# Order of the window sums and the turned maxima, and bank pairs of the score blocks, in an attention and convolution kernel on Trainium2

## The chip, the cores and the metric

The kernel runs on one core of one Trainium2 chip. TensorE (PE), VectorE (DVE), ScalarE (ACT), GpSimd (POOL) and SyncE (SP, which issues the transfers) each work through a queue of their own in program order and meet at semaphores. The metric is the device time of one launch in microseconds, the median of the runs.

## The reference, cut to what matters

```python
x = x + attention(gn(x))       # x is (4, 256, 32, 32): 4 images, 256 channels
x = x + conv(gn(x))

# attention: two halves of 128 channels
qkv = (windows(xh) @ h_qkv_w)                  # hifi: 2x2 windows, 4 tokens each, 4 heads of 32
attn = softmax(einsum('bghnd,bghmd->bghnm', q, k) * SCALE)      # 4 x 4 scores per window and head
hifi = einsum('bghnm,bghmd->bghnd', attn, v) @ h_proj_w + h_proj_b
q = xh @ l_q_w                                 # lofi: 1024 queries against 256 pooled keys, 4 heads
k, v = mean_2x2(xh) @ l_kv_w
lofi = softmax(q @ k.T * SCALE) @ v @ l_proj_w + l_proj_b

# conv: mask from each channel's centre of mass, then 3x3, 256 -> 256 channels
conv(x) = conv3x3(relu(x * mask(x)), weight) + bias
```

`gn` normalises over groups of 8 channels.

## The kernel before

The four images go through the same program one after the other. For image `b` the functions `front(b)` and `rest(b)` of each engine follow one another; the convolution of image `b-1` runs inside the attention of the next images: `Convolution(b).more(n)` issues the next `n` of its matmuls wherever TensorE would otherwise wait. The numbers of these matmuls stand in the tables `FRONT` and `REST`. `FRONT[2 + n]` come behind score block `n`, `FRONT[10]` (6) and `FRONT[11]` (10) around the window sums, `FRONT[12]` (23) behind the first pooled scores. Images 0 and 1 have no convolution to put there yet; in image 1 `keep_warm` issues filler matmuls behind blocks 5, 6 and 7 (6, 1 and 2 of them, two rows each in the trace).

The results of TensorE go to PSUM, which has four bank pairs here: `cps`, used by the convolution, and `slot[0]` to `slot[2]`, shared by all else. Each use of a pair waits by a semaphore until the reader of the one before is done.

The part that matters is the second half of `front(b)`:

- **Score blocks.** For each of 8 blocks of 128 queries TensorE makes the scores of 4 heads against 256 keys (L1185, four matmuls of 256 columns, `slot<-ks,qs` in the trace) into `slot[LA_SLOT[n]]`. VectorE takes the maxima over the keys (L782, `l_max<-slot`) and counts `la_max` up. Block `n` waits for the maximum that frees its pair.
- **Turned maxima.** TensorE transposes `l_max` (L1196, into `slot[2]`), VectorE copies it in two parts (`maxima_parts`, L790 and L792), and SyncE sends both to rows of `qs` (L280), where the pooled scores (`slot<-qs,ks`) need them.
- **Window sums.** GpSimd multiplies queries and keys of the windows (L348, `probs<-q_w,k_w`), TensorE sums the products over each head's channels (`window_scores`, `slot<-probs,cst`, 8 matmuls, 16 rows in the trace), ScalarE copies the sums (L542, `q_w<-slot`), TensorE transposes them (L1206, 8 transposes), and VectorE starts the softmax (`window_softmax`, L799 to L806) whose weights are turned back (L1229), copied by ScalarE as `p_w` (L556) and used for the values.
- **Convolution input of image `b-1`.** VectorE multiplies with the mask (`masked_image`, L722), ScalarE rectifies (L503, `rectify`), VectorE makes the tiles `v` (`conv_tiles`, L736 to L744) and their low parts (`conv_low`, L752, `v_lo`), ScalarE the high parts (L514, `v_hi`). TensorE's next convolution waits for both.

VectorE's order in `front` (L844) is written by hand: eight maxima, `maxima_parts`, a result of the older convolution, the two masked images, the first tiles, and then the window softmax.

Of the kernel before, what the change touches and what calls it, by code (L numbers as in the profile page):

```python
# [13 lines left out]
P = 128  # L14
B, C, H, W = 4, 256, 32, 32
KT = C // P
# [6 lines left out]
HEADS, HD = 4, 32  # L23
# [5 lines left out]
NB = HW // P  # L29
# [13 lines left out]
C_ID, C_GRP, C_HEAD, C_ONE = 0, P, 2 * P, 2 * P + HD  # L43
# [8 lines left out]
SPLITS = (slice(WLQ, WLK), slice(WLK, WCOLS), slice(WQ, WLQ))  # L52


LA_SLOT = (0, 1, 2, 0, 1, 2, 0, 1)
ST_SLOT = (0, 1, 0, 1, 1, 0, 2, 1)
PB_SLOT = (0, 1, 0, 2)

# [44 lines left out]
def build(nc, x, wqkv, whp, wlp, bh, bl, cw, cb, mw, filt, consts, selectors, out):  # L103
    with ExitStack() as ctx:
# [306 lines left out]
        def _(act):  # L411
# [23 lines left out]
            def input_moments(b, i):  # L435

                for k in range(KT):
                    act.wait_ge(x_in[b][k], 16)
                    channel_moments(b, 0, k, probs[:, i + k])
# [83 lines left out]
            def step(b, first, last):  # L523
                if first:
                    act.wait_ge(w_in, 3 * KT * 16)
                    nc.scalar.copy(w_hi[:], raw_w).then_inc(w_split, 1)
                    normalise_first()
                late = b + 1 == RING
                projections(b, first)
                if first:  # L530
                    act.wait_ge(cw_dve, CW_DVE)
                    weight_high(0, V_SUM, 2)
                    weight_high(0, V_DIFF, 0)
                if not first:
                    normalise_y(b - 1, b + 1)
                if not last and not late:
                    act.wait_ge(stacked_late, (b + 1) * STACK_LATE)
                    input_moments(b + 1, 0)
                if not first:
                    rectify(b - 1, 0)  # L540
                act.wait_ge(ssum_pe, b + 1)
                nc.scalar.copy(q_w[:], flat_cps if first else flat[0]).then_inc(ssum_sb, 1)  # L542
                if not first:
                    rectify(b - 1, 1)
                act.wait_ge(soft_c, b * N_SOFT + SOFT_READ)
                nc.scalar.activation(s_exp, s_exp, ACT.Exp, scale=SCALE).then_inc(sexp, 1)
                if not first:
                    conv_high(b - 1, 0)
                if not last and not late:
                    act.wait_ge(moments[0], (b + 2) * KT)  # L550
                exp_scores(b, range(2))
                if not first:
                    conv_high(b - 1, 1)
                    exp_scores(b, range(2, LT - NW))
                act.wait_ge(pt_pe, b + 1)
                nc.scalar.copy(p_w[:], flat[2]).then_inc(pt_act, 1)  # L556
                if first:
                    exp_scores(b, range(2, LT - NW))
                    act.wait_ge(cw_pool, CW_TURNED)
                    weight_high(1, V_SUM, 2)  # L560
                    weight_high(1, V_DIFF, 0)
                if late:
                    input_moments(b + 1, LT - NW)
                    act.wait_ge(moments[0], (b + 2) * KT)
                exp_scores(b, range(LT - NW, LT))
                if not last:
                    normalise(b + 1)
# [24 lines left out]
        def _(dve):  # L592
# [193 lines left out]
            def maxima_parts(b):  # L786

                dve.wait_ge(lmt_pe, b + 1)
                rows = slot[2][0:NB * HEADS, 0, 0:P]
                nc.vector.tensor_copy(lm_hi, rows).then_inc(lm_dve, 1)  # L790
                dve.wait_ge(lm_dve, b * 2 + 1)
                nc.vector.tensor_tensor(lm_lo, rows, lm_hi.bitcast(F32), ALU.subtract).then_inc(lm_dve, 1)  # L792
# [208 lines left out]
        def _(pe):  # L1001
# [120 lines left out]
            def front(b, conv, first=False):  # L1122

                starting = not first and isinstance(conv, NoConvolution)

                def tile_ready(k):
                    pe.wait_ge(xhi_ready, b * KT + k + 1)
                    pe.wait_ge(xlo_ready, b * KT + k + 1)


                project(slot[0], WLQ, tile_ready)
                if starting:
                    keep_warm(WARM[10])
                pe.wait_ge(pool_c, (b + 1) * N_POOL)
                if not first:
                    pe.wait_ge(y_ready, b * KT - 1)
                if first:
                    pe.wait_ge(w_split, 3)
                for k in range(KT):
                    split_mm(slot[1][:, 0, 0:G], (w_hi[:, k, WLK:WLK + P], w_lo[:, k, WLK:WLK + P]),  # L1140
                             (pool_hi[:, k], pool_lo[:, k]), k == 0, k == KT - 1)
                for t in range(MT):
                    m = slice(t * P, (t + 1) * P)
                    for k in range(KT):
                        ins = split_mm(slot[1][:, 1, m], (pool_hi[:, k, m], pool_lo[:, k, m]),
                                       (w_hi[:, k, WLV:WLV + P], w_lo[:, k, WLV:WLV + P]), k == 0, k == KT - 1)
                ins.then_inc(proj_pe, 1)
                if first:
                    pe.wait_ge(w_split, 4)
                else:  # L1150
                    pe.wait_ge(y_ready, b * KT)
                project(slot[2], WQ)
                pe.wait_ge(lq_dve, b + 1)
                project(slot[0], WK)
                conv.more(FRONT[0])
                if not first:
                    wait_count(pe, conv_out, (b - 2) * EVENTS + POS)
                    group_means(b - 1, 1)
                if not first:
                    pe.wait_ge(lk_act, (b + 1) * 2)  # L1160
                    pe.wait_ge(lk_dve, b + 1)
                    project(slot[1], WV)
                else:
                    project(cps, WV)
                conv.more(FRONT[1])

                for n in range(NB):
                    if n == 0:
                        pe.wait_ge(stacked, (b + 1) * STACK)
                        pe.wait_ge(qkv_sb, b * 3 + 2)  # L1170
                    elif n == 1:
                        if first:
                            pe.wait_ge(lk_act, 2)
                            pe.wait_ge(lk_dve, 1)
                        else:
                            pe.wait_ge(qkv_sb, b * 3 + 3)
                    elif n == 2:
                        if not first:
                            pe.wait_ge(gn_c[1], (b - 1) * N_GN + 1)
                    else:  # L1180
                        pe.wait_ge(la_max, b * NB + n - 2)
                    if n == NB // 2:
                        pe.wait_ge(stacked_late, (b + 1) * STACK_LATE)
                    for h in range(HEADS):
                        ins = mm(flat[LA_SLOT[n]][:, h * G:(h + 1) * G], qs[0:SC, h, n * P:(n + 1) * P], ks[0:SC, h],  # L1185
                                 True, True)
                    ins.then_inc(la_pe, 1)
                    conv.more(FRONT[2 + n])
                    if starting:
                        keep_warm(WARM[1 + n])  # L1190
                if first:
                    pe.wait_ge(qkv_sb, 3)
                    window_scores(b, cps)
                    pe.wait_ge(zeroed, 1)
                pe.wait_ge(la_max, (b + 1) * NB)
                nc.tensor.transpose(slot[2][:, 0, 0:P], l_max[:], cst[:, C_ID:C_ID + P]).then_inc(lmt_pe, 1)  # L1196
                conv.more(FRONT[10])
                if not first:
                    window_scores(b, slot[0])
                conv.more(FRONT[11])  # L1200

                pe.wait_ge(ssum_sb, b + 1)
                if not first:
                    pe.wait_ge(lm_dve, (b + 1) * 2)
                for n in range(NB):
                    ins = nc.tensor.transpose((cps if first else slot[2])[:, n // 4, (n % 4) * P:(n % 4 + 1) * P],  # L1206
                                              q_w[:, n * P:(n + 1) * P], cst[:, C_ID:C_ID + P])
                ins.then_inc(stok_pe, 1)

                if first:  # L1210
                    pe.wait_ge(ones, 1)
                pe.wait_ge(max_stacked, (b + 1) * MAX_STACK)
                for i in range(2):
                    pooled_scores(b, i)
                conv.more(FRONT[12])
                if not first:
                    Convolution(b - 1).more(EARLY)
# [155 lines left out]
```

## Time and profile before

| | us |
|---|---|
| median of 3 runs | 368.33 (368.22 to 368.52) |
| profiled execution | 366.82 |
| its span, first to last instruction | 364.9 |
| TensorE busy | 322.0 (88%) |
| VectorE busy | 280.5 (77%) |
| ScalarE busy | 148.0 (41%) |
| GpSimd busy | 85.8 (24%) |

The profiled execution took 1.9 us more than its span, and 1.5 us less than the median. Times in the rows below are from the start of the span. A matmul's row shows its modelled end, so rows of one engine overlap; the step from start to start is its pace. The mean granted clock of TensorE was 0.949 of full speed. Image 0's score blocks stand at 32 to 43 us, image 1's at 95 to 110, image 2's at 173 to 186 and image 3's at 249 to 261.

### The profile page before, as it was taken

How to read it: one execution, taken by the hardware profiler on the slowest of the kernel's cores; microseconds unless marked ns; L12 is line 12 of the kernel's file. 1: busy time of each engine (PE TensorE's matmuls, PEld its weight loads, DVE VectorE, ACT ScalarE, POOL GpSimd, SP SyncE). 2: the span in 40 equal slices, each digit the busy share in tenths (PEclk: the TensorE clock that was granted, in tenths of full speed). 3: DMA queues.
4: the chain of work that ended last, by engine and by line, in shares of the span. 5: the costliest groups of instructions: out<-in, count | busy, mean ns of one | idle time of the engine just before them, and what ended most of it. 6: DMA issues, size and time to landing. Idle time of an engine off the chain costs nothing.

```text
span 364.9 us, 4118 instructions
## 1 busy us (share of the span) xinstructions
PE 322.0 (88%) x1546; PEld 227.9 (62%) x1546; DVE 280.5 (77%) x518; ACT 148.0 (41%) x186; POOL 85.8 (24%) x47
## 2 busy tenths in 40 slices
PE   1786864999797699998999999998999999979995
PEld 1375542257564485486868773786777836858884
DVE  4979839777867957789897877988879847997662
ACT  2443556345443635535215764453048333031300
POOL 0464948000192020000760020005900200202000
PEclk9999698799968599999899999998999999999999
DMA  8659700007900000029510300098001000101002
GB/s 266 259 81 129 238 5 0 2 0 98 118 2 4 0 2 1 0 82 129 63 38 25 115 3 0 2 169 105 2 4 57 3 0 0 59 0 57 2 0 117
DMA packets 10340, 20.39 MB, mean 56 GB/s; under 512 B 1872, under 2 KB 4816, under 8 KB 10064
## 3 DMA queue, kind: packets, MB, share of 16 engines
q1 hardware_dynamic: 10320, 20.13, 26.8%
q8 instruction: 12, 0.20, 0.2%
q14 instruction: 8, 0.07, 0.1%
HBM read 7.93 MB, written 4.19 MB: 33 GB/s over the span
## 4 chain that ended last, share of the span: by engine, by line
PE 58%; DVE 17%; DMA 8%; ACT 6%; issue 4%; SPq 2%; POOL 2%; DVEq 0%
PE slot L1003 26%; PE cps L1035 16%; PE slot L1079 7%; DMA ks<-probs 4%; PE cps L1003 4%; DMA qs<-probs 3%; ACT probs L520 2%; PE cps L1079 2%; SPq L257 1%; DVE v_lo L752 1%; DVE xn L979 1%; SPq L261 1%; DVE l_max L782 1%; DMA xy<-x 1%; PE slot L1206 1%
## 5 line engine op out<-in xcount | busy, mean ns | idle before, releaser
L348 POOL TENSOR_TENSOR probs<-q_w,k_w 128x1024 f32<-128x1024 f32 x16 | 38.4, 2428 | 115.7 <-DVE rw L715 110.5
L1035 PE MATMUL cps<-v_hi,cw_hi 128*128 128x512 f32 (+1 forms) x144 | 58.6, 407 | 3.8 <-DVE v_lo L752 3.6
L1035 PE MATMUL cps<-v_hi,cw_lo 128*128 128x512 f32 (+1 forms) x144 | 58.4, 406 | 0.0
L1035 PE MATMUL cps<-v_lo,cw_hi 128*128 128x512 f32 (+1 forms) x144 | 57.4, 398 | 0.0
L782 DVE TENSOR_REDUCE l_max<-slot 128x4 f32<-128x1024 f32 x32 | 37.6, 1219 | 7.2 <-PE slot L1003 7.2
L520 ACT ACTIVATE probs<-slot 128x1024 f32<-128x1024 f32 x32 | 31.9, 1023 | 16.8 <-PE slot L1003 16.7
L1035 PEld LDWEIGHTS cps<-v_hi,cw_hi 128*128 128x128 f32 x144 | 28.3, 197 | 14.2 <-ACT v_hi L514 4.3
L1003 PE MATMUL slot<-ks,qs 96*128 96x256 f32 x128 | 24.9, 343 | 10.5 <-DVE l_max L782 4.4
L1035 PEld LDWEIGHTS cps<-v_hi,cw_lo 128*128 128x128 f32 x144 | 28.0, 194 | 6.3 <-issue 0.7
L1035 PEld LDWEIGHTS cps<-v_lo,cw_hi 128*128 128x128 f32 x144 | 28.1, 195 | 4.9
L1003 PEld LDWEIGHTS slot<-ks,qs 96*128 96x128 f32 x128 | 21.8, 236 | 14.4 <-DVE l_max L782 6.7
L503 ACT ACTIVATE xn<-mask 128x1024 f32<-128x1024 f32 x8 | 8.5, 1058 | 45.5 <-DVE mask L722 45.5
L1003 PE MATMUL slot<-xn_hi,w_hi 128*128 128x512 f32 x60 | 24.7, 411 | 2.3 <-DVE xn_lo L650 2.3
L333 POOL TENSOR_TENSOR mask<-rw 128x1024 f32<-128x1024 f32 x8 | 15.2, 1915 | 44.3 <-DVE rw L715 44.3
L1003 PE MATMUL slot<-qs,ks 98*128 98x512 f32 x64 | 21.0, 421 | 5.1 <-ACT probs L520 3.5
L514 ACT CAST v_hi<-mask 128x1024 fp32r<-128x1024 f32 x16 | 16.8, 1049 | 21.0 <-DVE mask L744 11.8
L1003 PE MATMUL slot<-xn_hi,w_lo 128*128 128x512 f32 x60 | 23.9, 398 | 0.0
L1003 PE MATMUL slot<-xn_lo,w_hi 128*128 128x512 f32 x60 | 23.7, 394 | 0.0
L392 POOL TENSOR_TENSOR q_w<-q_w,k_w 128x1024 f32<-128x1024 f32 x3 | 7.2, 2416 | 67.2 <-DVE k_w L885 67.2
L1003 PE MATMUL slot<-probs,cst 128*32 128x512 f32 x176 | 22.8, 657 | 0.0
L752 DVE TENSOR_TENSOR v_lo<-mask,v_hi 128x1024 fp32r<-128x1024 f32 x16 | 19.2, 1224 | 2.3 <-ACT v_hi L514 2.3
L1003 PE MATMUL cps<-cst 128*128 128x384 f32 x44 | 19.7, 602 | 0.0
(188 smaller groups left out, 623.2 us busy)
## 6 DMA issues: line engine op xcount, KB each, us to landing
qs<-probs SPq DMA_DIRECT2D x24, 256.0 KB, 7.5
xy<-x SPq DMA_DIRECT2D x8, 512.0 KB, 8.1
out<-xy SPq DMA_DIRECT2D x8, 512.0 KB, 2.8
raw_cw<-conv_w SPq DMA_DIRECT2D x2, 1152.0 KB, 6.9
ks<-probs SPq DMA_DIRECT2D x12, 128.0 KB, 7.4
probs<-h_qkv SPq DMA_DIRECT2D x2, 192.0 KB, 4.5
probs<-l_kv SPq DMA_DIRECT2D x2, 128.0 KB, 3.9
probs<-selectors SPq DMA_DIRECT2D x1, 256.0 KB, 4.0
```

The costliest lines, as they stand in the source:

```text
L257: sp.dma_start(qs[HD * part:HD * (part + 1), :, n].bitcast(F32), parts[:, n].bitcast(F32)).then_inc(done, 16)
L333: nc.gpsimd.tensor_tensor(mask[:, k].rearrange("p (h w) -> p h w", h=H), rw[:, k, 0].unsqueeze(2).to_broadcast([P, H, W]), rw[:, k, 1].uns ...
L348: nc.gpsimd.tensor_tensor(qk[:, j].rearrange("p (n w) -> p n w", n=NW), q_w[:].rearrange("p (n w) -> p n w", n=NW), k_w[:, j * G:(j + 1) * ...
L392: nc.gpsimd.tensor_tensor(pv[0], pv[0], pv[1], ALU.add).then_inc(pv_pool, 1)
L503: nc.scalar.activation(xn[:, k], mask[:, k], ACT.Relu).then_inc(relu, 1)
L514: nc.scalar.copy(v_hi[:, k, 2 * phase:2 * phase + 2].rearrange("p a b -> p (a b)"), mask[:, k]).then_inc(v_act, 1)
L520: nc.scalar.activation(probs[:, i], flat[score_slot(b, i)], ACT.Exp, scale=SCALE / NW)\
L752: nc.vector.tensor_tensor(v_lo[:, k, part].rearrange("p a b -> p (a b)"), mask[:, k], v_hi[:, k, part].rearrange("p a b -> p (a b)").bitca ...
L782: nc.vector.tensor_reduce(l_max[:, bass.ds(n, HEADS, step=NB)], flat[LA_SLOT[n]].rearrange("p (h m) -> p h m", h=HEADS), AX_X, ALU.max, ne ...
L1003: return nc.tensor.matmul(dst, lhsT, rhs, start=start, stop=stop)
L1035: ins = nc.tensor.matmul(cps[:, pos % 2, y0 * WT:y1 * WT], (cw_hi, cw_hi, cw_lo)[part][:, k, pos, dy + 1, o * P:(o + 1) * P], (v_hi, v_lo, ...
L1079: ins = nc.tensor.matmul(last_bank(o, pos)[:, y0 * WT:y1 * WT], (cw_hi, cw_hi, cw_lo)[part][:, k, pos, dy + 1, o * P:(o + 1) * P], (v_hi, ...
```

## The change

Three things are put in another order or place.

- `LA_SLOT`: blocks 5, 6 and 7 use the pairs 0, 1, 0 instead of 2, 0, 1. `LA_FREE` gives for each block the count of maxima that it waits for: 4 instead of 3 for block 5, 5 instead of 4 for block 6, 6 instead of 5 for block 7. So these three wait for the maximum of the block two before instead of three before.
- TensorE makes the window sums right behind the last block's convolution matmuls, into `slot[2]`, which block 2 was the last to use, and without a wait for the maxima. The transpose of `l_max` comes behind them and `FRONT[10]`, into `slot[1]`. The wait for `lm_dve` ahead of the sums' transposes goes.
- ScalarE copies the sums ahead of both rectifications, instead of between them.

```diff
-LA_SLOT = (0, 1, 2, 0, 1, 2, 0, 1)
+LA_SLOT = (0, 1, 2, 0, 1, 0, 1, 0)
+LA_FREE = (0, 0, 0, 1, 2, 4, 5, 6)
...
-                if not first:
-                    rectify(b - 1, 0)
                 act.wait_ge(ssum_pe, b + 1)
-                nc.scalar.copy(q_w[:], flat_cps if first else flat[0]).then_inc(ssum_sb, 1)
-                if not first:
-                    rectify(b - 1, 1)
+                nc.scalar.copy(q_w[:], flat_cps if first else flat[2]).then_inc(ssum_sb, 1)
+                if not first:
+                    for k in range(KT):
+                        rectify(b - 1, k)
...
-                rows = slot[2][0:NB * HEADS, 0, 0:P]
+                rows = slot[1][0:NB * HEADS, 0, 0:P]
...
-                        pe.wait_ge(la_max, b * NB + n - 2)
+                        pe.wait_ge(la_max, b * NB + LA_FREE[n])
...
                 if first:
                     pe.wait_ge(qkv_sb, 3)
-                    window_scores(b, cps)
                     pe.wait_ge(zeroed, 1)
+                window_scores(b, cps if first else slot[2])
+                conv.more(FRONT[10])
                 pe.wait_ge(la_max, (b + 1) * NB)
-                nc.tensor.transpose(slot[2][:, 0, 0:P], l_max[:], cst[:, C_ID:C_ID + P]).then_inc(lmt_pe, 1)
-                conv.more(FRONT[10])
-                if not first:
-                    window_scores(b, slot[0])
+                nc.tensor.transpose(slot[1][:, 0, 0:P], l_max[:], cst[:, C_ID:C_ID + P]).then_inc(lmt_pe, 1)
                 conv.more(FRONT[11])
 
                 pe.wait_ge(ssum_sb, b + 1)
-                if not first:
-                    pe.wait_ge(lm_dve, (b + 1) * 2)
```

In images 2 and 3 TensorE's queue behind the last convolution matmul of block 7 (`cps<-v_...` are convolution matmuls, `slot<-cst,l_max` is the transpose of the maxima, `slot<-probs,cst` the window sums) read before:

```order
L1196 MATMUL slot<-cst,l_max 128x128
L1035 MATMUL cps<-v_hi,cw_hi 128x512
L1035 MATMUL cps<-v_lo,cw_hi 128x512
L1035 MATMUL cps<-v_hi,cw_lo 128x512
L1035 MATMUL cps<-v_hi,cw_hi 128x512
L1035 MATMUL cps<-v_lo,cw_hi 128x512
L1035 MATMUL cps<-v_hi,cw_lo 128x512
L1003 MATMUL slot<-probs,cst 32x512 x8
L1035 MATMUL cps<-v_hi,cw_hi 128x496
```

and reads now:

```order
L1003 MATMUL slot<-probs,cst 32x512 x8
L1035 MATMUL cps<-v_hi,cw_hi 128x512
L1035 MATMUL cps<-v_lo,cw_hi 128x512
L1035 MATMUL cps<-v_hi,cw_lo 128x512
L1035 MATMUL cps<-v_hi,cw_hi 128x512
L1035 MATMUL cps<-v_lo,cw_hi 128x512
L1035 MATMUL cps<-v_hi,cw_lo 128x512
L1197 MATMUL slot<-cst,l_max 128x128
L1035 MATMUL cps<-v_hi,cw_hi 128x496
```

The sums moved up past the transpose and the six matmuls; the nine further convolution matmuls behind each are the same. In image 1, without a convolution, TensorE's queue from block 6 on is, before (- and + mark what goes and comes; `cps<-cst` are filler matmuls, `slot<-cst,q_w` the transposes of the sums):

```order
 L1003 MATMUL slot<-ks,qs 128x256 x4
 L1003 MATMUL cps<-cst 128x384 x2
-L1196 MATMUL slot<-cst,l_max 128x128
 L1003 MATMUL slot<-probs,cst 32x512 x8
-L1206 MATMUL slot<-cst,q_w 128x128 x8
+L1197 MATMUL slot<-cst,l_max 128x128
+L1202 MATMUL slot<-cst,q_w 128x128 x8
 L1003 MATMUL slot<-qs,ks 128x512 x4
 L1035 MATMUL cps<-v_hi,cw_hi 128x512
```

Only the transpose of the maxima changed places with the sums. VectorE's queue is unchanged in every image. In image 2 it reads from the last maxima to the softmax, before and now:

```order
L782 TENSOR_REDUCE l_max<-slot 128x4 x2
L790 CAST probs<-slot 32x128
L792 TENSOR_TENSOR probs<-slot,probs 32x128
L817 SCALAR_TENSOR_TENSOR xy<-cps,cbias,xy 128x512
L722 SCALAR_TENSOR_TENSOR mask<-mask,xn 128x1024 x2
L736 TENSOR_TENSOR mask<-xn 128x512
L737 TENSOR_TENSOR mask<-xn 128x512
L799 TENSOR_REDUCE s_max<-slot 128x32
```

Nothing moved there: the copy of the turned maxima (L790, the row with the wait for their transpose) stays ahead of the masked images (L722), the tiles (L736, L737) and the softmax (L799).

## Rows read from the trace of the kernel before

**Rows 1.** The page's chain that ended last, its shares by engine.

```profile
PE 58%; DVE 17%; DMA 8%; ACT 6%; issue 4%; SPq 2%; POOL 2%; DVEq 0%
```

**Rows 2.** That chain in order of time: start us, us, what; images 1 and 2.

```profile
122.64 4.79 PE cps L1035 x12
...
196.61 0.69 DVE mask L736
...
206.26 1.02 ACT p_w L556
207.32 0.74 PE slot L1003 x2
```

**Rows 3.** Timeline of TensorE, image 2: start us, us, engine, line, what.

```profile
173.68 2.35 PE L1003 MATMUL slot<-ks,qs 96*128 96x256 f32 x12 [1.79 <-DMA ks<-probs]
...
186.41 0.38 PE L1035 MATMUL cps<-v_hi,cw_lo 128*128 128x496 f32 x1
186.99 0.33 PE L1196 MATMUL slot<-cst,l_max 128*128 128x128 f32 x1 [0.20 <-DVE l_max L782]
187.07 0.48 PE L1035 MATMUL cps<-v_hi,cw_hi 128*128 128x512 f32 x1
...
188.63 1.94 PE L1003 MATMUL slot<-probs,cst 128*32 128x512 f32 x16
190.50 0.49 PE L1035 MATMUL cps<-v_hi,cw_hi 128*128 128x496 f32 x1
...
192.84 1.04 PE L1206 MATMUL slot<-cst,q_w 128*128 128x128 f32 x8
...
199.85 0.40 PE L1035 MATMUL cps<-v_hi,cw_hi 128*128 128x512 f32 x1
```

**Rows 4.** Timeline of VectorE, image 2; in brackets the idle time before.

```profile
187.35 0.28 DVE L790 CAST probs<-slot 32x128 fp32r<-32x128 f32 x1 [0.42 <-PE slot L1196]
...
188.71 2.35 DVE L722 SCALAR_TENSOR_TENSOR mask<-mask,xn 128x1024 f32<-128x1024 f32 x2
191.05 0.69 DVE L736 TENSOR_TENSOR mask<-xn 128x512 f32<-128x512 f32 x1
...
193.92 0.29 DVE L799 TENSOR_REDUCE s_max<-slot 128x32 f32<-128x128 f32 x1 [1.57 <-PE slot L1206]
```

**Rows 5.** Timeline of all engines, image 0.

```profile
35.43 9.20 DVE L782 TENSOR_REDUCE l_max<-slot 128x4 f32<-128x1024 f32 x8
...
38.78 3.75 PE L1003 MATMUL slot<-ks,qs 96*128 96x256 f32 x16 [1.35 <-DMA qs<-probs]
...
42.46 3.03 PE L1003 MATMUL cps<-probs,cst 128*32 128x512 f32 x16
...
49.43 1.16 PE L1003 MATMUL slot<-qs,ks 98*128 98x512 f32 x4 [1.66 <-DMA qs<-probs]
...
50.63 1.82 POOL L374 TENSOR_TENSOR raw_cw<-raw_cw 128x768 f32<-128x768 f32 x1 [4.65 <-DVE k_w L806]
```

**Rows 6.** Timeline of all engines, image 1.

```profile
111.74 0.33 PE L1196 MATMUL slot<-cst,l_max 128*128 128x128 f32 x1
...
113.86 1.06 ACT L503 ACTIVATE xn<-mask 128x1024 f32<-128x1024 f32 x1 [8.50 <-DVE mask L722]
114.82 0.99 ACT L542 COPY q_w<-slot 128x1024 f32<-128x1024 f32 x1
...
117.40 0.29 DVE L799 TENSOR_REDUCE s_max<-slot 128x32 f32<-128x128 f32 x1 [1.16 <-PE slot L1206]
...
122.64 0.77 PE L1035 MATMUL cps<-v_hi,cw_hi 128*128 128x512 f32 x1 [3.57 <-DVE v_lo L752]
```

**Rows 7.** Windows: length, busy of PE, PEld, DVE, ACT, POOL, granted clock, DMA.

```profile
49.00:51.00 2.00, 1.55 (x8) 1.07 (x9) 1.42 (x5) 0.77 (x1) 0.37 (x1) 1.00 0.01 4
44.00:45.50 1.50, 1.50 (x13) 0.29 (x5) 0.63 (x1) 0.46 (x2) 1.50 (x2) 0.76 0.02 8
174.50:176.00 1.50, 1.50 (x9) 1.50 (x8) 1.46 (x3) 0.71 (x1) 0.80 (x1) 0.50 1.08 123
```

More of the change, by code:

```diff
@@ L538, in step @@
                     input_moments(b + 1, 0)
+                act.wait_ge(ssum_pe, b + 1)
+                nc.scalar.copy(q_w[:], flat_cps if first else flat[2]).then_inc(ssum_sb, 1)
                 if not first:
-                    rectify(b - 1, 0)
-                act.wait_ge(ssum_pe, b + 1)
-                nc.scalar.copy(q_w[:], flat_cps if first else flat[0]).then_inc(ssum_sb, 1)
-                if not first:
-                    rectify(b - 1, 1)
+                    for k in range(KT):
+                        rectify(b - 1, k)
                 act.wait_ge(soft_c, b * N_SOFT + SOFT_READ)
```

## Prediction, written before the changed kernel ran

> **What bounds the kernel now.** I read the chain that ended last first. TensorE has 58% of it and VectorE 17% [rows 1], so neither engine's mean busy share answers the question: the chain changes engine inside every image, and the place where it changes is what counts. Followed in order of time through image 2 (images count from 0) it goes from TensorE over to VectorE (the softmax, then the second half of the convolution tiles at 196.61), from there to ScalarE (the turned weights' copy p_w at 206.26) and back to TensorE at 207.32 [rows 2]. What delays VectorE's softmax in an image therefore delays the end, one for one, until the end of p_w.
>
> Next I read the timeline of the two engines in that stretch. TensorE issues back to back: it waits 0.20 us for the last maximum before the transpose of l_max (186.99), then does six convolution matmuls from 187.07, the window sums from 188.63, ten convolution matmuls from 190.50 and the eight transposes at 192.84 [rows 3]. VectorE works by a fixed order. The copy of the turned maxima (187.35) stands before the masked images (188.71) and the first convolution tiles (191.05, two of 0.69), and only then comes the softmax, for which it waits 1.57 us at 193.92 [rows 4]. Image 3 has the same rows 75.6 us later, with the same wait of 1.57. These 1.57 us are all the room that VectorE has between the turned maxima and the softmax.
>
> **The change, part by part.**
>
> *The window sums go ahead of the turned maxima, images 2 and 3.* After the last block's five convolution matmuls TensorE no longer waits for the maximum. The last of the five starts at 186.41, so the sums can start at about 186.7 and take 188.63 to 190.50, which is 1.87; the six convolution matmuls take 187.07 to 188.63, which is 1.56 [rows 3]. The transpose of l_max then starts at about 186.7 + 1.87 + 1.56 = 190.1 instead of 186.99: 3.1 later. VectorE stands in front of exactly this transpose, and behind it in its queue are the two halves of the maxima, a convolution result, both masked images, the first tiles and the softmax. All of them move by 3.1, of which the wait of 1.57 covers half: the softmax starts 1.5 later, at 195.4 instead of 193.92 [rows 4]. The transposes of the sums themselves come 0.2 to 0.3 sooner, since the wait of 0.20 goes, but nobody can use that: VectorE is still at the tiles. The 1.5 go on down the chain. Convolution of the next image starts at 199.85, just behind v_lo [rows 3], so TensorE now waits there; the two transfers of the maxima are issued 3.1 later as well, and in image 0 TensorE had to wait 1.66 for their data at 49.43 [rows 5], so I expect part of this wait already before the pooled scores. Both waits are within the same 1.5, because p_w comes 1.5 late whatever TensorE does. Cost: **1.5 in image 2 and 1.5 in image 3**. It would be 1.2 each if TensorE's own wait alone counted (1.5 less the 0.3 won), and 1.6 if the transpose came 0.1 later.
>
> *The same in image 1.* There are no convolution matmuls here. The transpose of l_max stood at 111.74; now the sums stand before it, 1.9 by the same form, of which the end of the wait for the last maximum gives back 0.1. Behind the transpose VectorE has the same order and a wait of 1.16 before the softmax at 117.40 [rows 6]. To the 1.8 comes the delay of the blocks, next.
>
> *The last blocks alternate over two pairs.* Blocks 5, 6 and 7 now wait for the maximum of the block two before them, where they waited for that of the block three before. VectorE makes a maximum every 1.15 us (9.20 for eight) and a block at the low clock takes 0.94 (3.75 for sixteen rows, four each) [rows 5]. Two buffers thus just suffice to keep VectorE busy, since 0.94 and about 0.15 of hand-over are under 1.15, but TensorE loses its lead. In image 0 blocks 4 to 7 ran back to back from 38.78 to 42.53. Now block 7 starts behind the maximum of block 5, at 35.43 + 6 x 1.15 = 42.33, and ends at about 43.4: 0.85 later, and the window sums behind it too. The chain of image 0 runs from these sums over ScalarE's copy, the transposes at 46.68 and the softmax to GpSimd at 50.63, so it counts in full: **0.85 in image 0**. The bounds: the granted clock was 0.76 over 44 to 45.5 [rows 7], so it rose within the sums, which took 3.03 where the same form takes 1.94 at the full clock [rows 3, 5]. If it rises at the same moment as before, the later sums gain from it and 0.4 is left; if the new gaps between the blocks hold it down for all of them, they take 3.7 and it is 1.5.
>
> In image 1 the blocks before block 5 wait for VectorE already, so block 5 goes from behind one maximum to behind the next, 1.15 later. Twelve rows of filler matmuls come behind it, then blocks 6 and 7, with nothing that takes the 1.15 back; if the clock rises at its old moment, 0.6 of it remains. So the transpose of l_max comes 1.8 + 1.15 = 2.95 later, less the cover of 1.16: **1.8 in image 1** (1.2 to 2.3). TensorE stood 3.57 before the convolution at 122.64, waiting for v_lo [rows 6]: it will stand there 1.8 longer. In images 2 and 3 five convolution matmuls lie behind each block: these take 1.17 (half of the 2.34 from 190.50 to 192.84 [rows 3]), and with the block itself more than a maximum's 1.15, so the maximum is there before its block and the two pairs cost nothing. If this cover were gone it would be 1.15 again.
>
> *ScalarE copies the sums ahead of both rectifications.* In image 1 the copy stood at 114.82 behind a rectification of 1.06 (113.86), although the sums were there at about 111.74 + 0.25 + 1.94 = 113.9 [rows 3, 6]. Now the sums are themselves 0.7 later, so they are copied at 114.9 and the transposes start where they did. Worth nothing: both the copy and its 0.9 are covered by the late VectorE. In images 2 and 3 it is idle before the masked images anyway.
>
> *Moved at no cost:* the transpose of l_max into another bank pair, one of the two waits before the sums' transposes removed (the transpose of l_max no longer shares their pair), and the wait for the zeroed buffer.
>
> **Sum.** 0.85 + 1.8 + 1.5 + 1.5 = 5.65 us. The profiled execution took 366.8, so it would take 372.5; the median of the three runs stands 1.5 above it, 368.3, and gives 374.0.
>
> **The rivals.**
>
> *Smaller.* The two-pair waits of images 0 and 1 are hidden by a clock that rises as early as before (0.4 and 1.2), and TensorE's own wait alone counts in images 2 and 3 (1.2 each): 4.0, so 372.3; with the block waits fully hidden it is 371.3. For it: 1.15 against 0.94 plus hand-over is close. Against it: the rows of p_w make the chain pass over ScalarE, not TensorE.
>
> *Dearer, by the clock.* TensorE gets new gaps: between blocks 4 to 7 of image 0, and two of about 0.5 and 1.0 in each of images 2 and 3. A gap of 1.79 before 173.68 was followed by the low clock (0.50, which is 1.2 GHz, over 174.5 to 176); one of 1.66 before 49.43 was not (1.00, 2.4 GHz, over 49 to 51) [rows 3, 5, 7]. At the low clock twelve convolution matmuls take 4.79 [rows 2], at the full one ten take 2.34 [rows 3], so eight slow ones cost 1.3. If the clock falls, images 2 and 3 cost about 1.2 more each beyond TensorE's slack, and image 0 0.7 more: 8.7, so 377. The Trainium skill, "TensorE: Matmul & The Clock Gate", section "A second HAM failure mode: psum-queue depth-cycling", speaks against the change here: it tells of short idles between groups of matmuls that cycle through PSUM banks, which make the clock go up and down. By that rule this rival would be the forecast; the trace agrees with it only for the longer gap.
>
> *No change.* The late maxima are made up by a later wait that is not on the chain: for that p_w at 206.26 would have to be waited for less than the 1.5 it is late. TensorE went on 0.04 us after it (207.32 against 206.26 + 1.02 [rows 2]), so I give this little. 368.3.
>
> *Faster.* One mechanism: VectorE's room before the softmax is more than the transpose's delay of 3.1, and the sums' transposes set the softmax. Then image 1 gains the 0.95 of the copy, images 2 and 3 0.3 each, and image 0 still pays 0.85: 367.6. It decides at a wait of 3.1 at 193.92, and the trace has 1.57 [rows 4], at 117.40 1.16.
>
> **How the numbers follow.** Forecast (372.6 to 375.6) 0.62; smaller (370.5 to 372.6) 0.17; dearer (375.6 to 378) 0.15; no change 0.03; faster 0.03. The predicted time is the forecast's, 374.0. The range takes the forecast, the greater part of the smaller case and about half of the dearer one: 371.3 to 376.8. A measurement of this kernel tells about 0.2% from no change: faster 0.03, same 0.03, slower 0.94.
>
> **What would show it.** In the changed kernel's timeline the transpose of l_max starts behind the six convolution matmuls in images 2 and 3; VectorE waits some 3 us before the copy of the turned maxima and not at all before the softmax (the 1.57 is gone); the softmax starts 1.5 later against the first maximum of its image, 1.8 in image 1; TensorE waits about 1 us for v_lo before the next convolution, where it had no wait. Image 0: gaps of 0.2 to 0.4 between blocks 4 to 7 and the copy of the sums 0.85 later. I would be wrong if the softmax keeps a wait for TensorE, if p_w's lateness does not reach the image's end, or if the granted clock differs from before in the stretches after the new gaps.

## The result, and the profile after

The changed kernel took 373.49 us in the median of 6 runs (371.24 to 374.56), beside 368.27 us for the kernel before in the same session (365.52 to 368.81, 6 runs). The ratio is 1.017 [1.014, 1.020]: slower, by 5 to 7 us. The quotient of these two medians alone is 1.014; in the later sessions the kernel before had medians of 366.6 to 367.4, and against those the change costs 6.1 to 6.9. The profiled execution took 373.36 us with a span of 371.3, which is 6.4 more than the span before. The mean granted clock was 0.943.

The page of the changed kernel, its busy line and the shares of the chain that ended last:

```profile
PE 322.9 (87%) x1546; PEld 226.7 (61%) x1546; DVE 280.0 (75%) x518; ACT 148.8 (40%) x186; POOL 85.8 (23%) x47
...
PE 53%; DVE 25%; DMA 6%; ACT 6%; issue 4%; SPq 2%; POOL 2%; DVEq 0%
```

No engine works longer than before by more than 1 us. What moved is who is waited for: VectorE's share of the chain went from 17% to 25%, TensorE's from 58% to 53% [rows 1].

Image 2, timeline of TensorE in the changed kernel:

```profile
190.93 1.94 PE L1003 MATMUL slot<-probs,cst 128*32 128x512 f32 x16
192.81 0.51 PE L1035 MATMUL cps<-v_hi,cw_hi 128*128 128x512 f32 x1
...
194.31 0.27 PE L1197 MATMUL slot<-cst,l_max 128*128 128x128 f32 x1
...
196.66 1.04 PE L1202 MATMUL slot<-cst,q_w 128*128 128x128 f32 x8
198.16 1.20 PE L1003 MATMUL slot<-qs,ks 98*128 98x512 f32 x4 [0.47 <-DMA qs<-probs]
...
205.13 0.47 PE L1035 MATMUL cps<-v_hi,cw_hi 128*128 128x512 f32 x1 [0.52 <-issue]
```

And of VectorE in the same stretch:

```profile
189.92 1.23 DVE L782 TENSOR_REDUCE l_max<-slot 128x4 f32<-128x1024 f32 x1 [0.22 <-PE slot L1003]
194.62 0.28 DVE L790 CAST probs<-slot 32x128 fp32r<-32x128 f32 x1 [3.47 <-PE slot L1197]
...
195.14 0.73 DVE L817 SCALAR_TENSOR_TENSOR xy<-cps,cbias,xy 128x512 f32<-128x512 f32 x1
195.80 2.34 DVE L722 SCALAR_TENSOR_TENSOR mask<-mask,xn 128x1024 f32<-128x1024 f32 x2
198.13 0.69 DVE L736 TENSOR_TENSOR mask<-xn 128x512 f32<-128x512 f32 x1
...
199.34 0.28 DVE L799 TENSOR_REDUCE s_max<-slot 128x32 f32<-128x128 f32 x1
```

The last maximum is the point to measure from, since the queues ahead of it in the image are in their old order. Before, it started at 185.71, the copy of the turned maxima came 1.64 behind it and the softmax 8.21 [rows 4]. Now the copy comes 4.70 behind it, after a wait of 3.47, and the softmax 9.42, with no wait. So 3.06 go in, 1.85 are covered, and 1.21 come out. The covered part is the wait of 1.57 that is gone, 0.18 by which the masked images now follow the copy more closely (1.18 behind it, before 1.36 [rows 4]), and 0.10 by which the rows from the masked images to the softmax lie closer. Image 3 has the same rows 76.57 later, with the same 9.42.

The chain of the changed kernel in this stretch runs over that order:

```profile
191.00 1.87 PE slot L1003 x16
192.88 1.60 PE cps L1035 x6
195.14 0.73 DVE xy L817
195.87 2.27 DVE mask L722 x2
...
211.66 1.02 ACT p_w L556
212.72 0.73 PE slot L1003 x2
```

The sums and six convolution matmuls are on the chain, then VectorE's queue behind the turned maxima. `p_w` comes 21.74 behind the last maximum instead of 20.55 [rows 2], and TensorE still follows it after 0.04.

Image 0, all engines of the changed kernel:

```profile
35.32 9.69 DVE L782 TENSOR_REDUCE l_max<-slot 128x4 f32<-128x1024 f32 x8
...
38.66 5.08 PE L1003 MATMUL slot<-ks,qs 96*128 96x256 f32 x16 [0.85 <-DMA qs<-probs]
...
43.67 2.95 PE L1003 MATMUL cps<-probs,cst 128*32 128x512 f32 x16
...
48.93 0.29 DVE L799 TENSOR_REDUCE s_max<-cps 128x32 f32<-128x128 f32 x1 [1.42 <-PE cps L1202]
...
51.75 1.82 POOL L375 TENSOR_TENSOR raw_cw<-raw_cw 128x768 f32<-128x768 f32 x1 [5.89 <-DVE k_w L806]
```

The sixteen rows of blocks 4 to 7 take 5.08 instead of 3.75 [rows 5]. From the first maximum to the softmax it is 13.61 (12.38 before, from 35.43 to 47.81), so image 0 costs 1.23.

Image 1, all engines of the changed kernel:

```profile
99.91 5.74 DVE L782 TENSOR_REDUCE l_max<-slot 128x4 f32<-128x1024 f32 x5
...
104.58 1.22 PE L1003 MATMUL slot<-ks,qs 96*128 96x256 f32 x4 [1.04 <-DVE l_max L782]
105.59 6.53 PE L1003 MATMUL cps<-cst 128*128 128x384 f32 x12
111.67 0.93 PE L1003 MATMUL slot<-ks,qs 96*128 96x256 f32 x4
...
114.95 1.94 PE L1003 MATMUL slot<-probs,cst 128*32 128x512 f32 x16
116.83 0.33 PE L1197 MATMUL slot<-cst,l_max 128*128 128x128 f32 x1
...
117.19 0.28 DVE L790 CAST probs<-slot 32x128 fp32r<-32x128 f32 x1 [2.20 <-PE slot L1197]
...
121.25 0.28 DVE L799 TENSOR_REDUCE s_max<-slot 128x32 f32<-128x128 f32 x1
...
126.47 0.76 PE L1035 MATMUL cps<-v_hi,cw_hi 128*128 128x512 f32 x1 [3.78 <-DVE v_lo L752]
```

Here the softmax comes 21.34 behind the first maximum; before it was 18.55 (98.85 to 117.40 [rows 6]): 2.79. The parts, each from start to start: the filler matmuls begin 1.13 later against the first maximum, they take 6.08 until block 6 instead of 4.96 (+1.12), block 6 to the sums is 0.10 shorter, and the sums put 1.88 ahead of the transpose. That is 4.03, of which VectorE's old wait and its neighbours cover 1.24.

Both of these stretches lie where the clock changes level. Windows of before, in the columns of [rows 7]:

```profile
44.00:45.00 1.00, 1.00 (x12) 0.22 (x4) 0.63 (x1) 0.46 (x2) 1.00 (x2) 0.63 0.03 12
...
106.00:107.00 1.00, 1.00 (x4) 0.64 (x3) 0.00 (x0) 0.00 (x0) 1.00 (x2) 0.91 0.00 0
```

and of the changed kernel:

```profile
45.00:46.00 1.00, 1.00 (x8) 0.22 (x4) 0.01 (x1) 0.00 (x0) 0.86 (x1) 0.61 0.00 0
...
110.00:111.00 1.00, 1.00 (x4) 0.53 (x3) 0.00 (x0) 0.00 (x0) 1.00 (x1) 0.69 0.00 0
...
199.00:206.00 7.00, 6.49 (x29) 5.05 (x28) 6.37 (x13) 4.15 (x6) 0.00 (x0) 1.00 0.05 19
```

A window of 1 us with a mean of 0.63 held the level 1.00 for 0.26 of it, so the rise from 0.50 is at 44.74 before, and at 45.78 (0.61) now: 1.04 later, while the sums begin 1.21 later against the start of the span. So the sums paid nothing extra (2.95, before 3.03). In image 1 it is at 106.2 before (0.91) and at 110.6 now (0.69), which is 2.8 and 5.0 behind the start of the filler matmuls. Over the new gaps of image 2 (0.47 and 0.52) the clock stayed at 1.00.

The four images together give 1.23 + 2.79 + 1.21 + 1.21 = 6.44, and the span grew by 6.4. The stretches between these points differ as well, by 0.1 less ahead of image 0's first maximum, 0.1 less ahead of image 1's, 0.4 more from image 1's softmax to the last maximum of image 2 and 0.2 less from there on to that of image 3. These cancel, so the agreement to a tenth is in part luck.

### The profile page after: what moved, and what is told of

It reads as the page before. It is cut to its first block, busy times and chain, and to the rows that moved or that the text cites. A ratio compares the mean times of both kernels' runs of the same rounds, so it can differ in the third digit from the quotient of the medians.

```text
span 371.3 us, 4114 instructions
## 1 busy us (share of the span) xinstructions
PE 322.9 (87%) x1546; PEld 226.7 (61%) x1546; DVE 280.0 (75%) x518; ACT 148.8 (40%) x186; POOL 85.8 (23%) x47
## 4 chain that ended last, share of the span: by engine, by line
PE 53%; DVE 25%; DMA 6%; ACT 6%; issue 4%; SPq 2%; POOL 2%; DVEq 0%
PE slot L1003 25%; PE cps L1035 15%; PE slot L1079 7%; PE cps L1003 4%; DMA qs<-probs 3%; DVE l_max L782 3%; ACT probs L521 2%; DMA ks<-probs 2%; PE cps L1079 2%; DVE mask L722 2%; SPq L258 1%; DVE v_lo L752 1%; DVE xn L979 1%; DVE mask L737 1%; DVE mask L736 1%
## 5 line engine op out<-in xcount | busy, mean ns | idle before, releaser
L1003 PEld LDWEIGHTS slot<-qs,ks 98*128 98x128 f32 x64 | 11.9, 195 | 11.5 <-ACT probs L521 4.3
```

The costliest lines, as they stand in the source:

```text
L1003: return nc.tensor.matmul(dst, lhsT, rhs, start=start, stop=stop)
```

## The experiments

The theory was that two separate delays add: a block that waits for a bank pair in images 0 and 1, and VectorE's queue behind the late transpose of the maxima in images 1, 2 and 3. The rivals were that the clock in the new gaps makes the cost, that ScalarE's new order takes part, and that TensorE's own new waits (for the pooled data, for `v_lo`) count.

| kernel | median us | before, same session | ratio |
|---|---|---|---|
| order_only | 370.19 | 367.05 | 1.0087 [1.0059, 1.0115] |
| pairs_only | 371.76 | 367.05 | 1.0125 [1.0088, 1.0162] |
| copy_first | 366.47 | 367.05 | 0.9990 [0.9958, 1.0022] |
| turn_at_once | 371.86 | 367.05 | 1.0131 [1.0094, 1.0169] |
| twelve_ahead | 377.18 | 366.63 | 1.0283 [1.0254, 1.0311] |
| parts_late | 371.27 | 366.63 | 1.0121 [1.0090, 1.0152] |
| masked_ahead | 366.62 | 366.63 | 0.9994 [0.9967, 1.0022] |
| pairs_image0 | 368.96 | 367.43 | 1.0040 [1.0018, 1.0062] |
| pairs_image1 | 368.99 | 367.43 | 1.0040 [1.0015, 1.0065] |
| pairs_images23 | 367.20 | 367.43 | 1.0005 [0.9978, 1.0031] |

**Each part alone: order_only.** The kernel before, with the sums ahead of the turned maxima and ScalarE's copy first, but with three pairs to the end.

```diff
+                else:
+                    pe.wait_ge(la_max, b * NB + NB - 1)
+                    window_scores(b, slot[0])
+                conv.more(FRONT[10])
                 pe.wait_ge(la_max, (b + 1) * NB)
                 nc.tensor.transpose(slot[2][:, 0, 0:P], ...
-                conv.more(FRONT[10])
-                if not first:
-                    window_scores(b, slot[0])
```

> The window sums go ahead of the turned maxima as in the change, and ScalarE copies first, but the blocks keep three bank pairs (the sums stay in slot 0 behind block 6's maximum, the maxima are turned in slot 2). Theory (the late turned maxima hold VectorE, and the two pairs cost in images 0 and 1 alone): images 2 and 3 cost 3.0 less the cover of 1.66, 1.35 each, image 1 costs 1.8 less 1.16, 0.65, image 0 nothing: 3.3 over before, ratio 1.009. Rival (the alternation over two pairs is what costs, by way of the clock): no slower than before.

It cost 1.0087, 3.2 us, as expected. VectorE in image 2:

```profile
186.25 1.23 DVE L781 TENSOR_REDUCE l_max<-slot 128x4 f32<-128x1024 f32 x1 [0.22 <-PE slot L1002]
190.95 0.28 DVE L789 CAST probs<-slot 32x128 fp32r<-32x128 f32 x1 [3.47 <-PE slot L1199]
...
195.67 0.28 DVE L798 TENSOR_REDUCE s_max<-slot 128x32 f32<-128x128 f32 x1
```

These are the 4.70 and 9.42 of the changed kernel to the hundredth, so the cost of images 2 and 3 comes from the order, without the two pairs. Image 1 cost 0.44 here (18.99 from first maximum to softmax) and image 0 nothing (12.33).

**pairs_only.** The kernel before with the new `LA_SLOT` and `LA_FREE` and nothing else.

```diff
-LA_SLOT = (0, 1, 2, 0, 1, 2, 0, 1)
+LA_SLOT = (0, 1, 2, 0, 1, 0, 1, 0)
+LA_FREE = (0, 0, 0, 1, 2, 4, 5, 6)
...
-                        pe.wait_ge(la_max, b * NB + n - 2)
+                        pe.wait_ge(la_max, b * NB + LA_FREE[n])
```

> Only the bank pairs of blocks 5 to 7 and their waits are those of the change; the turned maxima stay ahead of the sums. Theory: image 0 costs 1.1, image 1 2.3 (half of it the wait, half the clock that rises later within the filler matmuls), images 2 and 3 nothing: 3.4 over before, ratio 1.009. With order_only it adds up to the 6.3 of the change. Rival (the order alone costs): 368, as before.

It cost 1.0125, 4.6 us, more than the 3.4 that were expected (the interval begins at 3.2). In images 2 and 3 it is the kernel before, with the wait of 1.57 and 8.22 from last maximum to softmax. Image 1 costs 1.12. Image 0 costs 2.80, more than in the changed kernel. Its TensorE there:

```profile
39.60 2.37 PE L1004 MATMUL slot<-ks,qs 96*128 96x256 f32 x8 [0.17 <-DVE l_max L783]
42.14 1.22 PE L1004 MATMUL slot<-ks,qs 96*128 96x256 f32 x4 [0.17 <-DVE l_max L783]
43.29 3.66 PE L1004 MATMUL cps<-probs,cst 128*32 128x512 f32 x16
...
48.11 1.97 PE L1207 MATMUL cps<-cst,q_w 128*128 128x128 f32 x8 [0.76 <-ACT q_w L543]
```

The gaps of 0.17 are the hand-overs; a block that starts alone takes 1.15 to the next instruction, where it took 0.92 (3.68 for four) back to back. The sums begin 8.35 behind the first maximum, as in the changed kernel, and 7.03 before: 1.32 for the waits. The other 1.5 is the clock: the sums ran low to their end (3.66, before 3.03) and the transposes ran low too (1.97, before 1.09). By their ratios the two parts come to 7.8, the whole change to 6.3, with intervals of 1.0 and 1.4 on the parts and 1.1 on the whole, so the runs leave open whether the parts add. In the spans of the profiled executions they do, 2.6 and 3.6 against 6.4. There pairs_only paid 1.5 for the clock in image 0 and nothing in its filler matmuls, and the changed kernel the other way round.

**copy_first.** The kernel before with ScalarE's new order only.

```diff
-                if not first:
-                    rectify(b - 1, 0)
                 act.wait_ge(ssum_pe, b + 1)
...
                 if not first:
-                    rectify(b - 1, 1)
+                    for k in range(KT):
+                        rectify(b - 1, k)
```

> Only ScalarE's order changes: the copy of the sums ahead of both rectifications. Theory: no change within 0.3 us; in images 2 and 3 the first rectification waits for the sums and comes 1.6 later, which the wait before the softmax just covers, in image 1 the softmax gains 0.2. Rival (the rectifications were the right thing to have first, and the change loses by it): 1 us or more slower.

No difference, 0.9990. VectorE takes 8.24 from last maximum to softmax in image 2, and 8.21 before. So ScalarE's order by itself does not cost; the interval is 1.2 us wide to either side. In the changed kernel ScalarE's copy of image 2's sums started at 192.97, 3.7 ahead of their transposes at 196.66, so the copy held up nobody there either.

**The dose: turn_at_once and twelve_ahead.** The changed kernel with 0 and with 12 convolution matmuls between the sums and the transpose of `l_max` instead of 6; the total stays.

```diff
-                conv.more(FRONT[10])
                 pe.wait_ge(la_max, (b + 1) * NB)
                 nc.tensor.transpose(slot[1][:, 0, 0:P], ...
+                conv.more(FRONT[10])
                 conv.more(FRONT[11])
```

> The changed kernel, but the transpose of the maxima stands right behind the sums, ahead of the six convolution matmuls. Theory (there is a cover of 1.6 in front of the softmax, and only what goes beyond it costs): in images 2 and 3 the transpose is now 1.5 late, inside the cover, so they cost nothing; what is left are the two pairs, 3.4, and image 1's 0.65: 4.0 over before, 2.4 less than the changed kernel. Rival (any place behind the sums costs in proportion to the delay): images 2 and 3 still cost 0.7 each, 5.4 over before.

```diff
-FRONT = (0, 0, 0, 0, 8, 5, 5, 5, 5, 5, 6, 10, 23)
+FRONT = (0, 0, 0, 0, 8, 5, 5, 5, 5, 5, 12, 4, 23)
```

> The changed kernel with twelve instead of six convolution matmuls between the sums and the transpose of the maxima, and four instead of ten behind it (images 2 and 3). Theory: the cover of 1.66 is used up already, so every further delay counts in full: the transpose comes 1.37 later (6 x 0.228), the softmax 1.37 later in each of the two images, 2.7 in all over the changed kernel, 9.0 over before, ratio 1.0245. With turn_at_once (0 in each) and the changed kernel (1.2 to 1.3 in each) it is the third point. Rival (it costs that the sums stand ahead, not how late the maxima are turned): as the changed kernel, ratio 1.017.

They took 1.0131 and 1.0283, with the change between them at 1.017: 4.8 and 10.4 us, where 4.0 and 9.0 were expected. VectorE in image 2, first of turn_at_once:

```profile
190.67 1.23 DVE L782 TENSOR_REDUCE l_max<-slot 128x4 f32<-128x1024 f32 x1 [0.22 <-PE slot L1003]
193.93 0.28 DVE L790 CAST probs<-slot 32x128 fp32r<-32x128 f32 x1 [2.03 <-PE slot L1196]
...
195.30 2.35 DVE L722 SCALAR_TENSOR_TENSOR mask<-mask,xn 128x1024 f32<-128x1024 f32 x2
...
198.86 0.28 DVE L799 TENSOR_REDUCE s_max<-slot 128x32 f32<-128x128 f32 x1
```

then of twelve_ahead:

```profile
190.08 1.23 DVE L782 TENSOR_REDUCE l_max<-slot 128x4 f32<-128x1024 f32 x1 [0.22 <-PE slot L1003]
196.11 0.28 DVE L790 CAST probs<-slot 32x128 fp32r<-32x128 f32 x1 [4.81 <-PE slot L1197]
...
200.83 0.28 DVE L799 TENSOR_REDUCE s_max<-slot 128x32 f32<-128x128 f32 x1
```

The copy comes 3.26 and 6.03 behind the last maximum, so 1.62 and 4.39 later than in the kernel before. The softmax stands 8.19 and 10.75 behind the last maximum, so 0.02 sooner and 2.54 later than its 8.21 before. For twelve_ahead this is the rule of the change again, 4.39 less a cover of 1.85. For turn_at_once the cover was 1.64, because there the masked images follow the copy by 1.37 as before, and not by 1.18; the delay of 1.62 just fits into it. VectorE had no wait left ahead of the softmax in either. So a delay within the cover costs nothing and one beyond it comes out whole, less a cover that itself differs by 0.2 between the kernels. Between the profiles of the change and of turn_at_once the spans differ by 1.5 only: the two images give 2.5 back, and the first maximum of image 0 stood 0.8 later in turn_at_once, ahead of all that was edited. twelve_ahead also waited 1.81 for the pooled data instead of 0.47, but the softmax was late in any case. Its median lost 3.7 against the changed kernel's, where two images explain 2.7; in its profile image 0 took 1.6 longer, as the clock stayed low through the sums (3.66) and their transposes (1.97).

**VectorE's queue: parts_late.** The changed kernel, but on VectorE the copy of the turned maxima and the convolution result stand behind the masked images.

```diff
                 maxima(b, range(6, NB))
-                maxima_parts(b)
-                older_result(V_DIFF)
...
                         masked_image(b - 1, k)
+                maxima_parts(b)
+                older_result(V_DIFF)
```

> The changed kernel, but VectorE's queue has the copy of the turned maxima behind both masked images (the transpose on TensorE stays late). Theory (it is VectorE's place behind the late transpose that costs): the masked images start right after the last maximum again. In images 2 and 3 the tiles and p_w come in time and only the maxima's data is late on TensorE, 0.5 to 0.8 each instead of 1.2 to 1.3; image 1 gains 2.0. With image 0's 1.1 that is 3.3 over before, ratio 1.009, 3.0 less than the changed kernel. Rival (TensorE's own order costs): within 1 us of the changed kernel.

It took 1.0121, 4.4 us over before, where 3.3 were expected. That is 1.8 less than the change, but the two intervals overlap, so the timeline has to decide. VectorE in image 2:

```profile
191.14 3.69 DVE L722 SCALAR_TENSOR_TENSOR mask<-mask,xn 128x1024 f32<-128x1024 f32 x2
...
194.75 0.27 DVE L790 CAST probs<-slot 32x128 fp32r<-32x128 f32 x1
...
197.81 0.29 DVE L799 TENSOR_REDUCE s_max<-slot 128x32 f32<-128x128 f32 x1 [0.60 <-PE slot L1203]
```

TensorE's transpose is as late as in the change, 4.39 behind the last maximum, but the masked images no longer stand behind it. The softmax comes 7.81 after the last maximum and waits 0.60 for the sums' transposes. `p_w` follows at 20.55 in image 2 and 20.68 in image 3, which were 20.55 and 20.57 before: at most 0.1 is left of the cost of images 2 and 3. The rest of the 4.3 by which the span is longer than before arose ahead of image 2: 2.8 in image 0, where the clock stayed low through the sums (3.66), 0.9 from there to image 1's first maximum and 0.3 in image 1. So a transpose as late as that costs next to nothing; what costs is what is queued behind it on VectorE. The later transfers and TensorE's waits take only the 0.40 that the softmax had won: `p_w` now waits 0.31 for TensorE.

**Both together, as a better version: masked_ahead.** The kernel before, three pairs, the sums ahead, the maxima turned right behind them, and VectorE's order of parts_late.

```diff
+                else:
+                    pe.wait_ge(la_max, b * NB + NB - 1)
+                    window_scores(b, slot[0])
...
-                nc.tensor.transpose(slot[2][:, 0, 0:P], ...
+                nc.tensor.transpose(slot[1][:, 0, 0:P], ...
...
-                if not first:
-                    pe.wait_ge(lm_dve, (b + 1) * 2)
```

> The kernel before (three pairs, ScalarE's old order) with the sums ahead, the maxima turned right behind them into slot 1, and VectorE's copy of them behind both masked images, so that nobody waits for the late transpose. Theory: image 1 gains 0.9, because the sums are copied and turned earlier than VectorE's tiles end, images 2 and 3 gain 0.2 to 0.4 each, as TensorE loses its wait for the last maximum: 1.5 less than before, ratio 0.996. Rival (the maxima's data, issued 2 us later, stops TensorE ahead of the pooled scores): 0.5 to 1 slower than before in each of images 1 to 3, ratio 1.005.

No measurable gain: 0.9994 [0.9967, 1.0022], where 0.996 was expected. In image 2 the softmax does come 0.44 sooner (7.77), but ScalarE's `p_w` stands 20.57 behind the last maximum, as before. The 0.44 is given back before `p_w`, which now waits 0.36 for TensorE. In image 1 the timeline does show the gain: the softmax comes 17.56 behind the first maximum (18.55 before) and the next convolution 22.79 (23.79 before). In this profile image 0 took 1.06 longer, 0.6 of it because the sums ran low (3.63 with three pairs), and the runs do not tell a gain of 1.0 from none: the interval reaches from 1.2 less to 0.8 more.

**The pairs, image by image.** `LA_SLOT` and `LA_FREE` of the change in the named images only, the kernel before otherwise.

```diff
+def la_slot(b, n):
+    return ((0, 1, 2, 0, 1, 0, 1, 0) if b in PAIR_IMAGES else (0, 1, 2, 0, 1, 2, 0, 1))[n]
```

> The kernel before, with blocks 5 to 7 on two bank pairs in image 0 alone. Theory: block 7 and the window sums come 0.85 to 1.2 later by the wait for the maximum, and where the granted clock stays low for all of the sums and their transposes another 1.6 comes on top, as in the profile of pairs_only: 1.2 to 2.8 over before, ratio 1.003 to 1.008. Rival (the cost lies in image 1): as before.

> The same in image 1 alone. Theory: the wait, 1.12 to 1.15, and up to 1.2 more where the clock rises late within the filler matmuls (as in the changed kernel's profile): 1.1 to 2.3 over before, ratio 1.003 to 1.006. Rival (the filler takes the wait up): as before.

> The same in images 2 and 3 alone. Theory: five convolution matmuls lie behind each block, the maximum is there before its block, nothing waits: as before, ratio 1.000. Rival (two pairs cost 1.15 in every image): 2.3 over before, ratio 1.006.

Image 0 alone and image 1 alone cost 1.5 us each (1.0040), images 2 and 3 nothing (1.0005). In the profile of pairs_image1 TensorE shows both parts of image 1's cost at once:

```profile
101.45 1.23 PE L1013 MATMUL slot<-ks,qs 96*128 96x256 f32 x4 [1.04 <-DVE l_max L792]
102.47 6.51 PE L1013 MATMUL cps<-cst 128*128 128x384 f32 x12
```

Its filler matmuls took as long as in the changed kernel. In pairs_only, with the same wait, they took 5.11. In the twelve profiles of this case, the fillers took 5.14 to 5.51 in the six kernels with three pairs in image 1; in the six with two they took 5.99 to 6.53 in four (the change, turn_at_once, twelve_ahead, pairs_image1) and 5.11 in two (pairs_only, parts_late). So the longer filler was seen only behind the new wait, but not always, and each kernel has one profile.

## Why the prediction was right

It said 374.0 and slower, with a range of 371.3 to 376.8; measured were 373.5. The sum of 5.65 stands against 6.4 in the profiled pair and 5.2 between the medians. The mechanisms were those named. The terms were off in both directions, images 2 and 3 by 0.6 too much and images 0 and 1 by 1.4 too little, so that the total came this close is in part luck.

- *Images 2 and 3, 1.5 each.* The transpose came 3.11 and VectorE's copy of it 3.06 later behind the last maximum (3.1 predicted), the wait in front of the softmax went, and nothing took its place. The cost was 1.21. The mis-sized term is the cover: 1.57 was read off the one wait before the softmax, and 1.85 was there, since the small gaps between the copy and the softmax close as well. The changed kernel and order_only show 1.85 alike, and twelve_ahead once more with another delay. That the value lies on the 1.2 given for TensorE's own wait alone is chance: that reasoning is not what happened, because parts_late keeps TensorE late and costs nothing there.
- *Two pairs in image 0, 0.85.* 1.32 by the start of the sums, 1.23 at the softmax, and the same 1.32 or 1.33 by the start of the sums in pairs_only, turn_at_once, twelve_ahead and parts_late (in pairs_image0 the sums begin 1.9 later, where block 4 had waited 1.95 for a transfer). VectorE did not keep its pace of 1.15: it waits at the hand-overs too, so that eight maxima take 9.69 instead of 9.20, and block 7 alone took 1.15 (pairs_only) where 1.07 was counted. The hand-over of 0.15 was taken to fit between two maxima, and it did not.
- *Image 1, 1.8.* 2.79. The pair wait (1.13 for 1.15) and the sums ahead of the transpose (1.88 less 0.10, for 1.8) were right, and the cover was 1.24 (for 1.16). The missing term is 1.12 of filler matmuls at the low clock: the prediction had the clock rise at its old moment or earlier, as a gain, and in this execution it rose later. The kernels order_only (5.32 for the filler rows) and pairs_only (5.11) did not pay it, pairs_image1 (6.51) did.
- *Two pairs in images 2 and 3, nothing.* Shown by pairs_images23.
- *ScalarE's order and the removed wait, nothing.* Shown for the order by copy_first. The removed wait was not tried by itself.
- *Smaller.* Neither half of it came about: no wait of images 0 and 1 was hidden by an earlier rise in the changed kernel, and in images 2 and 3 its 1.2 was met by another way, as said.
- *What would show it.* The wait of some 3 us before the copy (3.47) and none before the softmax were there. The wait before the next convolution was 0.52 and not 1: TensorE was itself held 0.47 by the pooled data ahead of it. In image 0 the gaps were 0.17 (pairs_only), not 0.2 to 0.4, and the copy of the sums came 1.24 later.
- *Dearer, by the clock.* Its mechanism did not come about in images 2 and 3, where it was placed: 1.00 over 199 to 206. It did in part in images 0 and 1, where the clock was low already and rose later: 1.1 in image 1 here, 1.5 in image 0 in pairs_only. By the prediction's own sign of being wrong, a clock that differs behind a new gap, this is where it fell short: image 1's filler matmuls follow the new wait of 1.04. The Trainium skill, "TensorE: Matmul & The Clock Gate", section "A second HAM failure mode: psum-queue depth-cycling", tells of a kernel in which short idles between groups of matmuls toggle the clock. The traces agree with it for none of the gaps of 0.47 to 0.52 at full clock. With gaps of 0.17 in image 0 the sums ran low to the end in three of the profiles with two pairs (3.66), but pairs_image1 and masked_ahead, with three pairs there, also had 3.65 and 3.63, so no run here shows that the gaps are the cause. What only kernels with two pairs in image 0 had, in three of six profiles, is that the transposes of the sums ran low as well (1.97). The longer gap, where the prediction had the trace agree with that section, does not hold up: the kernel before has 1.79 ahead of image 2's blocks and the low clock behind it [rows 3, 7], the changed kernel 1.88 ahead of image 3's and 1.00 behind it (the last rows of this document).
- *No change* and *faster*: VectorE's cover was 1.85 and not 3.1, and `p_w` passed its lateness on, as it was argued.

Open is what sets the moment at which the clock rises in images 0 and 1. It decides about 1.1 to 1.5 us in each, as much as the pair waits, and may be why pairs_only cost 4.6 where the two single images give 3.0; the intervals of the two overlap, so the difference may also be noise.

## What to carry to other kernels

When an instruction is moved back in one engine's queue, look at what is queued behind its consumer on the other engine: the cost is the delay less all the waits from that consumer to the first instruction that the chain needs, here 3.06 less 1.85, and nothing while the delay stays below them. Putting independent work ahead of the consumer made the same delay all but free. A buffer ring of two cost nothing where other work lies behind each use, and cost both the hand-overs and the overlap of successive blocks where none does.

## What the runs showed of the hardware

- The same instructions ran at different clocks from profile to profile (one profile of each of twelve kernels that differ little ahead of these rows). Image 1's twelve filler rows took 5.11 to 6.53 us, and image 0's sixteen rows of sums 2.81 to 3.66; in the windows shown the level was 0.50 up to a rise whose moment differed. From one profile, a term of 1 us that lies over such a rise can't be forecast to better than its own size.
- A faster clock gave little where a transfer was behind it. In image 3 the changed kernel ran blocks 0 to 2 at the full clock (1.70 for twelve rows, clock 1.00 over 253 to 256), and then waited 1.02 for the next part of `qs`, a wait that the kernel before, at the low clock there, did not have. The last maximum came 11.75 behind the first block, before 12.03, so 0.3 was left of it. TensorE of the changed kernel:

```profile
254.74 1.70 PE L1003 MATMUL slot<-ks,qs 96*128 96x256 f32 x12 [1.88 <-DMA ks<-probs]
...
260.90 0.71 PE L1003 MATMUL slot<-ks,qs 96*128 96x256 f32 x4 [1.02 <-DMA qs<-probs]
```
